# A decoder's attention with row-packed scores: the order of key strips in shifts and exponentials, and the place of row scores beside shifts

## The reference

```python
att = einsum('bqhd,bkhd->bhqk', q, k) / sqrt(8)      # cross: clip(att, -1e4, 1e4); causal: hide k > q
att = softmax(att, axis=-1)
out = einsum('bhqk,bkhd->bqhd', att, v).reshape(B, L, D) @ Wo + bo
x = x + out
```

## Time and profile before

| | us |
|---|---|
| median of 3 runs (lowest, highest) | 1382.79 (1382.32, 1399.76) |
| span of the profiled execution | 1375.2 |
| TensorE busy | 1177.9 (86%) |
| VectorE busy | 880.0 (64%) |
| GpSimd busy | 777.3 (57%) |
| ScalarE busy | 676.7 (49%) |

### The profile page before, as it was taken

How to read it: one execution, slowest core, us unless ns; L and a number is a source line. 1 busy time by engine, 2 the same in 40 slices (tenths; PEclk the granted TensorE clock), 3 DMA queues, 4 the chain that set the end, 5 groups by cost and what they waited for, 6 DMA issues and landing times. The chain is left out here.

```text
span 1375.2 us, 34181 instructions
## 1 busy us (share of the span) xinstructions
PE 1177.9 (86%) x12731; PEld 892.8 (65%) x12731; DVE 880.0 (64%) x2024; ACT 676.7 (49%) x1304; POOL 777.3 (57%) x878
## 2 busy tenths in 40 slices
PE   1899998888888876999879999994799998499992
PEld 0577776655555555666547777773699996388882
DVE  3688877579999885766446666663689876322223
ACT  1344544435445432555345545545778753156551
POOL 3787775546555642444366556642666776765452
PEclk9999999689999998899969999997799998599996
DMA  9920000000000000000000000000000001466665
GB/s 346 380 86 2 2 3 8 9 15 15 19 17 15 9 10 1 1 1 1 1 1 2 2 2 3 2 3 19 12 7 13 11 23 32 127 215 204 194 193 187
DMA packets 51571, 75.46 MB, mean 55 GB/s; under 512 B 13118, under 2 KB 31683, under 8 KB 51152
## 3 DMA queue, kind: packets, MB, share of 16 engines
q1 hardware_dynamic: 43344, 60.57, 13.5%
q0 software_dynamic: 4544, 8.47, 1.8%
q10 hardware_dynamic: 3520, 4.23, 0.9%
HBM read 40.37 MB, written 31.70 MB: 52 GB/s over the span
## 5 line engine op out<-in xcount | busy, mean ns | idle before, releaser
L597 DVE TENSOR_REDUCE maxes<-bank 128x8 f32<-128x1024 f32 x192 | 234.4, 1221 | 52.8 <-PE bank L396 51.2
L524 ACT ACTIVATE self_probs<-bank 128x1024 f32<-128x1024 f32 x128 | 129.1, 1022 | 45.9 <-PE bank L428 45.5
L1475 POOL DMA_INDIRECT returned<-relu_y,relu_slots x78 | 76.3, 979 | 68.0 <-DVE relu_y L1451 53.4
L1412 ACT ACTIVATE relu_hidden<-bank,cols 128x256 f32<-128x256 f32 x156 | 73.8, 473 | 76.8 <-PE bank L1371 76.8
L531 ACT ACTIVATE self_neg_max<-bank 128x512 fp32r<-128x512 f32 x64 | 38.2, 596 | 148.3 <-PE bank L442 148.3
L738 POOL TENSOR_TENSOR self_k_hi_m<-self_kq_hi,const 128x512 fp32r<-128x512 f32 x64 | 66.5, 1038 | 78.5 <-ACT self_kq_hi L552 78.5
L1371 PE MATMUL bank<-latent_kq,relu_w_tile 128*128 128x256 f32 x312 | 94.4, 385 | 0.5 <-DVE latent_kq L1445 0.5
L1379 PE MATMUL bank<-relu_hidden,relu_w_tile 128*128 128x256 f32 x312 | 93.0, 381 | 0.0
L607 DVE RECIPROCAL self_recip<-bank 128x128 f32<-128x128 f32 x64 | 61.2, 956 | 30.9 <-PE bank L455 28.6
L1445 DVE COPY latent_kq<-bank 128x256 f32<-128x256 f32 x39 | 16.6, 425 | 99.7 <-PE bank L1361 94.9
L603 DVE TENSOR_SCALAR bank<-bank 128x1024 f32<-128x1024 f32 x64 | 78.2, 1223 | 3.3 <-PE bank L416 3.2
(11 more groups left out here) (395 smaller groups left out, 3470.8 us busy)
## 6 DMA issues: line engine op xcount, KB each, us to landing
relu_w_tile<-in_w_ffn SPq DMA_DIRECT2D x39, 512.0 KB, 3.5
routed<-blank SPq DMA_DIRECT2D x1, 19760.0 KB, 61.2
relu_slots<-routed SPq DMA_DIRECT2D x39, 130.0 KB, 3.2
x_all<-in_x SPq DMA_DIRECT2D x8, 256.0 KB, 8.3
x_before<-x_all SPq DMA_DIRECT2D x8, 256.0 KB, 2.3
relu_back<-returned SPq DMA_DIRECT2D x4, 512.0 KB, 8.0
latent_mask_rows<-returned ACTq DMA_DIRECT2D x4, 512.0 KB, 8.5
self_ctx_in<-in_ctx SPq DMA_DIRECT2D x8, 192.0 KB, 2.5
```

What stands on the lines that cost most here:

```text
L524: act.activation(probs[n % 2][:, 2 * pair:2 * pair + 2, :, :].rearrange("p u j q -> p (u j q)"), T[:, 2 * pair * GT:(2 * pair + 2) * GT], ...
L597: dve.tensor_reduce(out.rearrange("p j u -> p u j"), S.rearrange("p (u j k) -> p u j k", u=2, j=U), AX.X, ALU.max, negate=True).then_inc(m ...
L1412: act.activation(hidden[i % C1][:, :], HT[i % 2][:, 0:TT], ACT.Relu, bias=sb["cols"][:, bass.ds(r + (COL_RELU + c), 1)]).then_inc(hidden_d ...
L1475: pool.indirect_dma_start(returned[:, :], bass.IndirectOffsetOnAxis(ap=slots[t % NX][:, b, P:P + 1].bitcast(I32), axis=0), y[t % NY][:, b, ...
```

## The change

Two things. First, the code: a function `key_strips` says that the first pair of shifts, clips and exponentials (f0, x0, e0) belongs to strips 2 and 3, and the second (f1, x1, e1) to strips 0 and 1. T's passes go over the strips in the order 2, 3, 0, 1. The row scores keep their strips: s0 has 0 and 1, s1 has 2 and 3. Second, the table: in self, ScalarE does e0 ahead of m, and TensorE has q ahead of f1 (f1 then stands directly before s1). In causal, TensorE has k ahead of s0, f0 directly behind T, x directly behind y, and f1 directly behind s1; ScalarE does kh and e0 ahead of m. The lines of cross stay.

```diff
     "causal": {
-        "PE": "s0 k^5 T m y f0 s1 x^6 f1 w q^5 v^4",
-        "ACT": "m kh^5 e0 xh^6 e1 k^6 q^5 ln^7 qh^4",
+        "PE": "k^5 s0 T f0 m y x^6 s1 f1 w q^5 v^4",
+        "ACT": "kh^5 e0 m xh^6 e1 k^6 q^5 ln^7 qh^4",
...
+        def key_strips(pair):
+
+            return (2, 3) if pair == 0 else (0, 1)
...
-                for u in range(U):
+                order = key_strips(0) + key_strips(1)
+                for u in order:
                     pe.matmul(out[u], k_hi[rows_of(u), batch_cols(n)], q_hi[rows_of(u), :, :],
                               start=not causal, stop=False)
-                for u in range(U):
+                for u in order:
                     pe.matmul(out[u], k_hi[rows_of(u), batch_cols(n)], q_lo[rows_of(u), :, :], start=False, stop=False)
-                for u in range(U):
+                for u in order:
                     mm = pe.matmul(out[u], k_lo[rows_of(u), batch_cols(n)], q_hi[rows_of(u), :, :],
                                    start=False, stop=clip)
...
-                for u in (2 * pair, 2 * pair + 1):
+                for u in key_strips(pair):
                     mm = pe.matmul(t_bank(u), cr[rows_of(u), C_ONES + u * P:C_ONES + (u + 1) * P],
                                    neg_max[n % 2][rows_of(u), :], start=False, stop=True, skip_group_check=clip)
...
-                act.activation(probs[n % 2][:, 2 * pair:2 * pair + 2, :, :].rearrange("p u j q -> p (u j q)"),
-                               T[:, 2 * pair * GT:(2 * pair + 2) * GT], ACT.Exp, scale=scale).then_inc(exp_done, 1)
+                u = key_strips(pair)[0]
+                act.activation(probs[n % 2][:, u:u + 2, :, :].rearrange("p u j q -> p (u j q)"),
+                               T[:, u * GT:(u + 2) * GT], ACT.Exp, scale=scale).then_inc(exp_done, 1)
...
-                t = T[:, 2 * pair * GT:(2 * pair + 2) * GT]
+                u = key_strips(pair)[0]
+                t = T[:, u * GT:(u + 2) * GT]
```

## The result

The changed kernel takes 1406.68 us (median of 14 runs, 1394.22 to 1419.23). The kernel before, run 14 times beside it, takes 1387.09 (1377.01 to 1399.76). The ratio is 1.0121, with a 95% interval from 1.0093 to 1.015: slower by 1.2%. The forecast was 1379.7, with a range up to 1400.

What follows compares the result with a forecast made beforehand. TensorE was taken to bound causal, VectorE cross, and VectorE's maximum the s0-to-s1 path in self. Causal -5.1, self -1.3 and clock +3.3 gave -3.1 us, so 1379.7 from 1382.8; range 1364 to 1400.

Steps and rivals of the forecast that it cites:

- f0 and f1, plain batch: Causal: f0 behind T saves its 0.43 us, f1 beside s1 saves a pass of 0.24.
- f0 and f1, batch with kh: Causal, 6 batches with kh: the same savings, 0.43 us for f0 and 0.24 for f1.
- x waits for the addition: Causal, 6 batches: x behind y waits for the addition emptying its bank, 0.45 us each, 2.7 lost.
- k ahead of s0: Causal: saves a change of row grouping, 0.19 x 6 = 1.1 us won, between 0 and 2.6.
- e0 ahead of the copy: Causal: w waits for the copy of the maxima, 0.09 us in 18 batches, 1.6 lost.
- kh ahead of the copy: Causal, 6 batches: kh waits for f1, delaying the copy and w by 2.30 us each, 13.8 lost.
- clock, falls at the new waits: Causal: TensorE's idle at the new waits brings two short clock falls, 3.3 us lost, bounds 0 and 30.
- first two distances of causal: First T to next batch's first T, causal's first two; no cost of their own was taken.
- rival 3: Causal: the clock falls at every new wait and stays low for 10 us; 1406.4 us, chance 0.15.
- the 1.3 us that were taken for self: Self, 6 batches with x: e0 ahead of m lets T start 0.21 us earlier, 1.3 won.
- rival 2: Causal: strips don't run apart, so f0 pays its pass of 0.24 us; 1385.8 us, chance 0.17.
- Rival 1: Causal: the kh wait doesn't bite because the copy comes in time; 1362.6 us, chance 0.13.

Runs made afterwards that it cites:

- run 14: Not a run's label: the words say that the kernel before was run 14 times beside the changed one, median 1387.09 us.
- copy first: Changed kernel with ScalarE's causal line as before, so the copy of the maxima precedes kh and e0: 1366.73 us, ratio to before 0.9798.
- all ahead: Changed kernel with self's old order; in causal the copy, then e0, then kh, and x behind f1: 1365.57 us, ratio 0.9783; again 1365.23, 0.9826.
- scores first: Kernel of all ahead with k behind s0 again in causal: 1362.83 us, ratio to before 0.98.
- filled wait: Changed kernel plus nine matmuls of unused result ahead of w in the six batches with kh: 1390.62 us, ratio to before 1.0028.
- strips only: Changed code and strips with both order tables of the kernel before: 1376.82 us, ratio to before 0.9883.
- old strips: Kernel of all ahead with the first pair of shifts and exponentials on strips 0 and 1 again: 1381.15 us, one profile.

## Why the prediction was wrong

The steps of the prediction, with what the runs gave (causal; gains negative):

| step | taken | measured |
|---|---|---|
| f0 and f1, plain batch | -0.67 (0.43 + 0.24) | -0.67 (6.24 to 5.57, copy first) |
| f0 and f1, batch with kh | -0.67 | -0.44 (41.5 to 38.9 in 6, copy first) |
| x waits for the addition, each of 6 | +0.45 | +0.48 idle; 0.62 saved by x behind f1 (all ahead) |
| k ahead of s0, each of 6 | -0.19, bounds 0 to -0.43 | -0.41 (scores first) |
| e0 ahead of the copy, plain batch | +0.09 | +0.22 (copy first) |
| kh ahead of the copy, each of 6 | +2.30 | +2.29 (filled wait) |
| clock, falls at the new waits | +3.3 in all | +11.2 in all, w's later start included (filled wait) |
| first two distances of causal | no cost of their own, so -1.2 | +3.8 |

The forecast was 3.1 us less, and the ratio of 1.0121 makes it 16.8 more: 19.9 us to account for. Causal has 17.5 of them (-1.8 taken with the clock, +15.7 measured) and self 1.3; the rest is within the spread of the stages outside. Of causal's 17.5, the clock has 7.9, the first two distances 5.0, e0 ahead of the copy 2.1, the batches with kh 1.4.

**The step that failed first of all is the clock.** The prediction took two short falls on the ground that "Around the new waits TensorE is denser than there", meaning where the clock had fallen in the earlier trace rows. The runs show a fall at every one of the six waits, in both profiles of the changed kernel. Five lasted 3.41 us and one 6.83, as long as the short kind of fall that was taken (3.3), so the price of one was nearly right, 11.2 / 6 = 1.9 against 1.65, and their number was wrong: six, not two. This is rival 3 with short falls; by its own rule (falls at every wait) with the price of the short kind, 6 x 1.65, the forecast would have been 1386.3 us, and with the measured one 1387.6. So the clock alone does not bring the forecast to the measured time; that rival 3's own figure, 1406.4, came so near it is luck, since no fall of 10 us followed these waits.

**The second step that failed is k ahead of s0, counted only inside causal's steady batches.** There it gains, 0.41 us in each of six, more than was taken. Its price stands ahead of the first T and in the first two batches, where no row was looked at. The stage between the last T of cross and the first of causal took 201.2 and 205.1 us in two profiles of before, 210.9 and 210.8 in two of the changed kernel. Scores first lays 2.7 us of this (15.91 against 13.25) and 2.9 to 4.0 us of the first two distances at k's place, in the version with all steps ahead; the changed kernel itself was not run with k's place alone undone. The rest is not settled: strips only, with k behind s0, took 205.1 between the stages as well.

**Two smaller terms were mis-sized to the same side.** The way from the copy's end to w was taken as 0.14 us, the distance between an exponential's end and T. In the plain batch of the changed kernel the copy runs from 827.48 for 0.59 us and w starts at 828.33, 0.26 later; so e0 ahead of the copy costs 3.7 us in all, not 1.6. The passes saved in a plain batch came out as taken, but the batches with kh saved 2.6 us in all where 6 x 0.67 = 4.0 was taken. In these batches T had not run beside s0 before, since k stood between the two, and its strips started together:

```profile
822.30 0.46 PE L411 MATMUL bank<-causal_q_hi_m,causal_kq_hi 32*128 32x512 f32 x4
```

From there to m at 823.15 it took 0.85 us, not 1.06. With f0 in between it takes 1.07 as in every batch (copy first), so f0's 0.43 are won and 0.22 of them lost again.

**What was right.** The mechanisms named for causal's steady batches stood where they were said to, the wait for the copy (2.29 us against 2.30) first of all. f0 runs beside T's last pass: the strips do run apart, so rival 2 falls. On this the Trainium skill, "TensorE: Matmul & The Clock Gate", Part 3 on packing small matmuls, says that matmuls start in program order; the row of L416 at 831.16, ahead of the last two L385 at 831.27, disagrees with it, as the earlier trace rows did. Rival 1 falls too: w waits for the copy in all six. In self, s1 is still tied to the maximum (1.72 us); the batch with x gained the 0.21 us that were taken, but from the strips and not from e0. Two of the other three batches of a group lost 0.10 each: one with the strips alone as well (6.62 to 6.72), the other only with e0 ahead of m (6.32 to 6.42). So four batches take 25.39 us as before (25.38), and the 1.3 us that were taken for self did not come. Cross shows no change beyond its spread: from its first T to its last 245.6 and 244.7 us before, 242.3 and 246.7 in the changed kernel.

## What to carry to other kernels

When a step moves ahead of another on an engine's queue, the question is what it waits for, not how long it takes: kh (0.63 us) is needed by nobody for a long time, and put ahead of the copy it handed its own wait for f1 to TensorE. In a stage where TensorE is never idle, a new wait like these is to be priced as the wait plus the lower clock behind it, at each place where it stands, until a trace shows otherwise. And a line of steps that is shared by a stage's first iterations and its steady ones has to be costed in both: k ahead of s0 gains 0.41 us per group in the one, 2.5 in all, and in the other it costs at least as much (2.7 us ahead of the first T, 2.9 to 4.0 behind it).

## What the runs showed of the hardware

- TensorE stood still ahead of w six times in causal, 2.36 to 2.53 us, and the clock fell at each of the six, during the wait or up to 1.0 us behind its end, in both profiles; with matmuls in the same stretch whose results nobody read, no time out of six.
- The falls came in few lengths: 3.41 and 6.83 us at the waits, at the head of causal 23.9 us in all four profiles with k behind s0 (before twice, strips only, scores first), and with k ahead 41.0 in five of eight, 34.1 in two (filled wait and the first run of all ahead) and 47.8 in one (old strips). Why the clock came back later there, by the 1.41 us of idle or by what ran after it, is open.
- Matmuls on disjoint strips pass each other: a pair of passes on strips 2 and 3 started 0.24 us into a pass that the program issues over all four strips ahead of it, whichever strips that pass began with.
